# Probability blocks turned by VectorE in 32x32 squares and through a scratch tensor in HBM

## What is computed

```python
h = _layernorm(x, axis=-1) * (1 + ca) + sa          # x: (2, 1024, 256)
qkv = jnp.einsum('bsh,ph->bsp', h, weight_qkv).reshape(b, s, NKV, GROUP)
scores = jnp.einsum('bsgqd,btgd->bgqst', q, k) * scale
scores = jnp.where(causal, scores, jnp.finfo(scores.dtype).min)
attn = jax.nn.softmax(scores, axis=-1)
out = jnp.einsum('bgqst,btgd->bsgqd', attn, v)
x = x + ga * jnp.einsum('bse,he->bsh', out, weight_proj)
```

## Time and profile before

| | us |
|---|---|
| median of three runs | 979.47 (979.19 to 979.89) |
| the profiled execution, its own time | 979.04 |
| its span, first to last instruction | 977.2 |
| PE, PEld busy in the span | 947.1, 816.0 |
| DVE, ACT, POOL busy in the span | 653.1, 516.6, 467.7 |
| mean granted TensorE clock | 0.997 of full |
| DMA over the span | 22 GB/s |

### The profile page before, as it was taken

One profiled execution on the slowest core, in us unless ns is written; L12 is line 12 of the kernel. 1 busy time (PEld: TensorE's weight loads), 2 busy tenths in 40 slices (PEclk: granted clock), 3 DMA queues, 4 the chain that ended last, 5 costly groups with the idle time before them and its releaser, 6 DMA issues.

```text
span 977.2 us, 14506 instructions
## 1 busy us (share of the span) xinstructions
PE 947.1 (97%) x5344; PEld 816.0 (83%) x5344; DVE 653.1 (67%) x1290; ACT 516.6 (53%) x1085; POOL 467.7 (48%) x603
## 2 busy tenths in 40 slices
PE   6899999999999999999999999999999999999997
PEld 5688888888898889888988898889888987888885
DVE  6777657775777577757775777567757776864553
ACT  2466646664666466646664666466646665331221
POOL 3665646564556455545654565456545656120000
PEclk9999999999999999999999999999999999999999
DMA  8000000100010001000000010001000020000000
GB/s 313 24 1 33 2 22 1 33 1 22 1 33 2 22 1 33 1 23 1 33 1 22 1 33 1 22 1 34 1 1 1 1 87 1 1 8 15 21 21 21
DMA packets 9666, 21.92 MB, mean 22 GB/s; under 512 B 1280, under 2 KB 5504, under 8 KB 9472
## 3 DMA queue, kind: packets, MB, share of 16 engines
q1 hardware_dynamic: 8736, 20.45, 6.2%
q10 hardware_dynamic: 864, 0.60, 0.2%
HBM read 18.96 MB, written 2.10 MB: 22 GB/s over the span
## 4 chain that ended last, share of the span: by engine, by line
PE 80%; DVE 9%; ACT 5%; POOL 3%; issue 2%; DMA 1%; SPq 0%; DVEq 0%; POOLq 0%; ACTq 0%
PE ps L801 17%; PE ps L803 16%; PE ps L802 16%; PE ps L924 10%; PE ps L903 6%; PE ps L909 6%; PE ps L906 6%; ACT prob L487 2%; POOL rinv L373 2%; DVE pt_lo L706 2%; POOL prob L378 2%; DVE xhat L614 1%; DVE ps L702 1%; PE ps L825 1%; DVE v_lo L681 1%
## 5 line engine op out<-in xcount | busy, mean ns | idle before, releaser
L706 DVE TENSOR_TENSOR pt_lo<-ps,pt_hi 128x512 fp32r<-128x512 f32 x288 | 198.0, 690 | 101.7 <-ACT pt_hi L506 98.9
L506 ACT ACTIVATE pt_hi<-ps 128x512 fp32r<-128x512 f32 x288 | 171.0, 597 | 134.1 <-PE ps L924 132.6
L373 POOL TENSOR_TENSOR rinv<-rsum,mone 128x1 f32<-128x1 f32 x256 | 140.7, 550 | 211.5 <-ACT prob L487 210.7
L378 POOL TENSOR_SCALAR prob<-prob,rinv 128x1024 f32<-128x1024 f32 (+7 forms) x256 | 192.2, 751 | 53.3 <-POOL rinv L373 53.3
L487 ACT ACTIVATE prob<-ps,nmax 128x1024 f32<-128x1024 f32 (+7 forms) x256 | 189.5, 741 | 50.0 <-DVE nmax L702 48.3
L702 DVE CUSTOM_DVE_ANT_0 ps<-ps,mask_f 128x1024 f32<-128x1024 f32 (+7 forms) x256 | 192.9, 765 | 21.8 <-PE ps L909 19.5
L924 PE MATMUL ps<-ident,prob 128*128 128x128 f32 x1152 | 175.1, 273 | 6.2 <-DVE pt_lo L706 3.6
L924 PEld LDWEIGHTS ps<-ident,prob 128*128 128x128 f32 x1152 | 140.3, 140 | 36.8 <-DVE pt_lo L706 10.9
L801 PE MATMUL ps<-pt_hi,v_hi 128*128 128x512 f32 x288 | 132.5, 460 | 1.3 <-DVE pt_lo L706 0.5
L803 PE MATMUL ps<-pt_hi,v_lo 128*128 128x512 f32 x320 | 126.3, 395 | 0.0
L903 PE MATMUL ps<-k_hi,q_hi 128*128 128x512 f32 (+4 forms) x384 | 117.6, 360 | 0.0
(11 more groups left out here) (134 smaller groups left out, 1575.8 us busy)
## 6 DMA issues: line engine op xcount, KB each, us to landing
w_raw<-in_wqkv SPq DMA_DIRECT2D x9, 768.0 KB, 4.2
wp_raw<-in_wproj SPq DMA_DIRECT2D x8, 512.0 KB, 3.5
x<-in_x SPq DMA_DIRECT2D x4, 512.0 KB, 9.8
prob<-in_wug SPq DMA_DIRECT2D x4, 512.0 KB, 5.3
out_y<-prob SPq DMA_DIRECT2D x4, 512.0 KB, 3.0
prob<-in_wmod SPq DMA_DIRECT2D x1, 1024.0 KB, 9.7
raw_down<-in_wdn SPq DMA_DIRECT2D x1, 1024.0 KB, 14.1
prob<-in_wmod SPq DMA_DIRECT2D x1, 512.0 KB, 5.2
```

The source lines that it names most:

```text
L378: g_.tensor_scalar(row, row, rinv[:, s % 2, h:h + 1], 1.0, ALU.mult, ALU.mult).then_inc(prob_done, 1)
L506: a_.activation(pt_hi[:, n % 3, :], T[n % 2], ACT.Copy).then_inc(pth_done, 1)
L706: v_.tensor_tensor(pt_lo[:, n % 3, :], T[n % 2], pt_hi[:, n % 3, :].bitcast(F32), ALU.subtract).then_inc(ptl_done, 1)
```

## The change

In rows 7, 6 and 5 the last four units (`SWAPPED`, 12 of 36) are no longer transposed by TensorE. For each head of such a row VectorE transposes 32x32 squares of the last four blocks from `prob` into `blocks` (X in the order, placed by a planner `BEHIND` units of its clock after the head's scores). When all four heads are there, SP stores `blocks` (128x2048 numbers) to `spill` in HBM, waits for it, and reads it back in four loads, one for each 32 partitions, which brings the squares to their places in `swapped` (two buffers). In the order such a unit is E instead of T: ScalarE makes `pt_hi` from `swapped` (the first of a row waits for the loads), GpSimd makes `pt_lo`. On ScalarE the held exponentials run after E's work. `pt_hi` and `pt_lo` have four buffers. GpSimd now follows `WALK`, and splits the weights after row 4, head 3. `raw_down` and the butterflies' buffers share memory with `swapped` and `blocks`; the load of `wdn` and its first butterflies move to the end of the last turn.

```diff
+QB = 32
+NB = P // QB
+SWAP_ROWS = [7, 6, 5]
+GROUP = 4
+SWAPPED = [n for n, (i, j) in enumerate(UNITS) if i in SWAP_ROWS and j > i - GROUP]
+TURNED = [n for n in range(NU) if n not in SWAPPED]
...
-    return out
+    return with_blocks([("E", n, 0) if what == "T" and n in SWAPPED else (what, n, h) for what, n, h in out])
+BEHIND = 3300
+WEIGHTS_AFTER = 4
+def with_blocks(walk):
+    cost = {"C": 1360, "VT": 900, "L": 1000, "T": 443, "V": 680, "Y": 1400, "E": 0}
+    out, open_blocks, now = [], [], 0
+    for what, n, h in walk:
+        while open_blocks and now >= open_blocks[0][0]:
+            out.append(open_blocks.pop(0)[1])
+        out.append((what, n, h))
+        now += 160 * (n + 1) if what == "S" else cost[what]
+        if what == "S" and n in SWAP_ROWS:
+            open_blocks.append((now + BEHIND, ("X", n, h)))
+    return out + [block for _, block in open_blocks]
...
+                    for r, i in enumerate(SWAP_ROWS):
+                        at = group(t, i)
+                        sp.wait_ge(block_done, this(block_done, t, QPG * (r + 1)))
+                        if at >= 2:
+                            sp.wait_ge(el_done, len(SWAPPED) + (at - 1) * GROUP)
+                        sp.dma_start(spill[at % 2, :, :], blocks[:, :]).then_inc(spill_s[at % 2], 16)
+                        sp.wait_ge(spill_s[at % 2], (at // 2 + 1) * 16)
+                        for kb in range(NB):
+                            sp.dma_start(swapped[kb * QB:(kb + 1) * QB, at % 2, :].rearrange("p (a n) -> p a n", a=NB),
+                                         spill[at % 2, :, kb * GROUP * P:(kb + 1) * GROUP * P].rearrange(
+                                             "(a p) n -> p a n", a=NB)).then_inc(swap_s[at % 2], 16)
...
+                    def swapped_low(n):
+                        pool.wait_ge(eh_done, this(eh_done, t, SWAPPED.index(n) + 1))
+                        g_.tensor_tensor(by_head(pt_lo, n), swapped_tile(t, n), by_head(pt_hi, n).bitcast(F32),
+                                         ALU.subtract).then_inc(el_done, 1)
+                    for what, i, h in WALK:
+                        if what == "E":
+                            swapped_low(i)
+                        if what == "S":
+                            normalise(i, h)
+                        if what == "S" and (i, h) == (WEIGHTS_AFTER, QPG - 1):
                             pool.wait_ge(wraw_s, (t + 2) * 16)
...
+                        if what == "E":
+                            i, j = UNITS[n]
+                            if n >= 4:
+                                act.wait_ge(pv_done, this(pv_done, t, n - 3))
+                            if j == i - GROUP + 1:
+                                act.wait_ge(*landed(group(t, i)))
+                            a_.activation(by_head(pt_hi, n), swapped_tile(t, n), ACT.Copy).then_inc(eh_done, 1)
                             exps()
...
+                        if what == "X":
+                            s = NT - 1 - n
+                            at = group(t, n)
+                            if h == 0 and at:
+                                dve.wait_ge(spill_s[(at - 1) % 2], ((at - 1) // 2 + 1) * 16)
+                            dve.wait_ge(prob_done, this(prob_done, t, QPG * s + h + 1))
+                            v_.transpose(blocks[:, :].rearrange("p (k j h q) -> p j k h q", k=NB, j=GROUP, h=QPG)[:, :, :, h, :],
+                                         prob[:, s % 2, h, (n + 1 - GROUP) * P:(n + 1) * P].rearrange(
+                                             "p (j k q) -> p j k q", j=GROUP, k=NB)).then_inc(block_done, 1)
...
+                            if n in SWAPPED:
+                                pe.wait_ge(el_done, this(el_done, t, SWAPPED.index(n) + 1))
+                            else:
+                                pe.wait_ge(ptl_done, this(ptl_done, t, turned(n) + 1))
```

More of the change, by code:

```diff
@@ L87, in halves, with build @@
     return (2, n // 2) if n > CH else (1, n)
-def build(nc, x_in, wqkv, wproj, wmod, c_cols, wug, wdn, su_ug, su_dp, ws_ug, ws_dp, ident_in, mask_in, had_in, out):
+def build(nc, x_in, wqkv, wproj, wmod, c_cols, wug, wdn, su_ug, su_dp, ws_ug, ws_dp, ident_in, mask_in, had_in, out, spill):
     ctx = ExitStack()
@@ L109, in build @@
         prob = sb("prob", [P, 2, QPG, SEQ])
-        pt_hi = sb("pt_hi", [P, 3, CH], F32R)
-        pt_lo = sb("pt_lo", [P, 3, CH], F32R)
+        pt_hi = sb("pt_hi", [P, 4, CH], F32R)
+        pt_lo = sb("pt_lo", [P, 4, CH], F32R)
+        blocks = sb("blocks", [P, GROUP * CH])
+        swapped = sb("swapped", [P, 2, GROUP * CH])
+        raw_down = swapped[:, 0, :]
+        sum_dn, dif_dn = (blocks[:, n * 4 * HID:(n + 1) * 4 * HID].rearrange("p (a k n) -> p a k n", a=2, k=KH)
+                          for n in range(2))
         o_hi = sb("o_hi", [P, 2, CH], F32R)
@@ L233, in build, with turned, group, landed @@
         CHUNKS += [("q", h, 1) for h in range(QPG)] + [("q", h, 0) for h in range(QPG)]
+        def turned(n):
+            return TURNED.index(n)
+        def group(t, i):
+            return t * NG + SWAP_ROWS.index(i)
+        def landed(g):
+            return swap_s[g % 2], (g // 2 + 1) * 16 * NB
+        def swapped_tile(t, n):
+            i, j = UNITS[n]
+            tile = swapped[:, group(t, i) % 2, :].rearrange("p (a j h q) -> p a j h q", a=NB, j=GROUP, h=QPG)
+            return tile[:, :, j - i + GROUP - 1, :, :].rearrange("p a h q -> p h a q")
+        def by_head(pt, n):
+            return pt[:, n % 4, :].rearrange("p (h a q) -> p h a q", h=QPG, a=NB)
         def bank(c):
@@ L295, in _ @@
                                  wqkv[bass.ds(g + 1, 1), :, :].rearrange("a p (k n) -> p (a k) n", k=KH)).then_inc(wraw_s, 16)
-            wide = sum(i + 1 for i in STEPS if i >= CT)
+                    for r, i in enumerate(SWAP_ROWS):
[9 more added lines that the diff above has]
+                                             "(a p) n -> p a n", a=NB)).then_inc(swap_s[at % 2], 16)
+            sp.wait_ge(el_done, (TURNS + 1) * len(SWAPPED))
+            sp.dma_start(raw_down, wdn).then_inc(raw_s[4], 16)
+            wide = len([n for n in TURNED if UNITS[n][0] >= CT])
             sp.wait_ge(t_done, this(t_done, TURNS - 1, wide))
@@ L367, in _, with normalise @@
                     ln_low(1, b, g, 0)
[L368 to L379, removed]
+                    def normalise(i, h):
+                        s = NT - 1 - i
+                        e = QPG * s + h
+                        pool.wait_ge(exp_done, this(exp_done, t, e + 1))
+                        g_.tensor_tensor(rinv[:, s % 2, h:h + 1], rsum[:, s % 2, h:h + 1], mone[:, :],
+                                         ALU.pow).then_inc(rinv_done, 1)
+                        pool.wait_ge(rinv_done, this(rinv_done, t, e + 1))
+                        pool.sem_inc(pool_gate, 1)
+                        row = prob[:, s % 2, h, 0:(i + 1) * P]
+                        g_.tensor_scalar(row, row, rinv[:, s % 2, h:h + 1], 1.0, ALU.mult, ALU.mult).then_inc(prob_done, 1)
+                    def swapped_low(n):
[8 more added lines that the diff above has]
+                        if what == "S" and (i, h) == (WEIGHTS_AFTER, QPG - 1):
                             pool.wait_ge(wraw_s, (t + 2) * 16)
@@ L387, in _ @@
                                              ALU.subtract).then_inc(w_ready, 1)
+                        if t == TURNS - 1 and what == "S" and (i, h) == (2, QPG - 1):
+                            pool.wait_ge(raw_s[4], 16)
+                            g_.tensor_tensor(sum_dn, a[:, :, :, 0, :], a[:, :, :, 1, :], ALU.add)
+                            g_.tensor_tensor(dif_dn, a[:, :, :, 0, :], a[:, :, :, 1, :], ALU.subtract).then_inc(fly_s, 1)
             def raw_high(n):
@@ L938, in _ @@
                                 pe.wait_ge(v_lo_s, this(v_lo_s, t, 2))
-                            pe.wait_ge(ptl_done, this(ptl_done, t, n + 1))
-                            three(O[s], v_hi[:, j, :], v_lo[:, j, :], pt_hi[:, n % 3, :], pt_lo[:, n % 3, :],
+                            if n in SWAPPED:
+                                pe.wait_ge(el_done, this(el_done, t, SWAPPED.index(n) + 1))
+                            else:
+                                pe.wait_ge(ptl_done, this(ptl_done, t, turned(n) + 1))
+                            three(O[s], v_hi[:, j, :], v_lo[:, j, :], pt_hi[:, n % 4, :], pt_lo[:, n % 4, :],
                                   j == 0, j == i).then_inc(pv_done, 1)
```

42 lines of the change are left out of this document (22 added, 20 removed).

## The result

| | us |
|---|---|
| changed kernel, median of 4 runs | 1195.3 (1194.04 to 1199.72) |
| kernel before, beside it | 979.33 |
| ratio | 1.2214 (95%: 1.218 to 1.2248) |
| the profiled execution: its own time, its span | 1194.25, 1192.5 |
| mean granted TensorE clock | 0.891 of full (before 0.997) |

The kernel is 216 us slower. The forecast of 1176 was 19 us too low, and the range held the time. First the page: busy time and instructions of each engine, the granted clock in 40 slices of the span (before, 9 in all 40), the chain by engine, three new groups, and the transfers.

A forecast was written before the change was run, and what follows sets the result against it. TensorE, busy for 97% of the span, was taken to bound the kernel. 979 + 198 (eight turns of 30.4 us of waits less 5.6 saved) - 1 for the ends = 1176 us; range 1100 to 1222.

The forecast's parts named there:

- the removal: On TensorE, 96 transposed units at 0.44 us go, 42.2 us; with short waits a turn would be 5.6 us shorter.
- Prices of the new work: Per unit: VectorE's square transposes 0.7 us (highest bound 2.2), ScalarE's upper half 0.65, GpSimd's lower half 1.30.
- The trip: A row's 1 MB to HBM and back: write 4.6 us, read 7.0, together 11.6, bounds 9.3 to 13.5.
- rival 1: Loads into 32 partitions keep the full rate: read 5.6 instead of 7.0 us, 34 us less, 1142; chance 0.18.
- half rate: Loads into 32 partitions run at half the rate: 2.8 us more, read 8.4, kernel 1210; chance 0.15 with beyond.
- The waits: TensorE's waits at swapped units in rows 7, 6 and 5: 30.4 us a turn against 5.6 saved, 198 us in eight.
- The ends: Butterflies moved from start to last turn: up to 3.7 us gained at the start, 2.6 lost later, together -1.
- Full rate: Loads into 32 partitions not slowed: read 5.6 instead of 7.0 us, three trips a turn, 1142 us; chance 0.18.
- Slow squares: VectorE's square transposes take 2.2 us instead of 0.7: 36 us on the chains, 1212 or more; chance 0.08.
- Short trip: Write and read take 5 us together, only the orders remain: 12.8 - 5.6 = 7.2 us a turn, 1036; chance 0.12, shared with too strict an order.
- Faster: Swapped units are split before TensorE reaches them, waits under 5.6 us a turn; fully hidden 933 us; chance 0.02.
- No saving: The removed transposes cost TensorE nothing: 979 + 243 - 1 = 1221 us; chance 0.02.

The follow-up runs named there:

- b4_two_units: Changed kernel swapping only the last two units of the three rows, held exponentials ahead of E's work, weights split after row 3: 967.49 us, ratio 0.9893.
- b1_straight: Changed kernel whose four loads each write 512 columns of all 128 partitions instead of 2048 columns of 32; output not the reference's: 1147.18 us.
- a1: Changed kernel with GpSimd splitting the next turn's weights after row 3, head 3 instead of row 4, head 3: 1154.59 us.
- a2: Changed kernel with ScalarE running the held exponentials before E's work instead of behind it: 1148.61 us.
- a3: Changed kernel with both the later weight split and the exponentials ahead of E's work: 1100.05 us.
- c4_filled: Changed kernel with transposes that nobody reads put on TensorE ahead of the waits at five swapped units: 1162.22 us.
- a4_small: Changed kernel with store and loads moving an eighth of the bytes, instructions and orders kept, output not the reference's: 1112.83 us.
- b2_putback: Changed kernel in which TensorE makes the 12 units' transposes again at E, into a free bank that nobody reads: 1193.86 us.

## Why the prediction was right, and where it was short

**What bounds the kernel, and the removal.** Transposes at 0.44 us a unit were on the path before; `b4_two_units` shows the gain where little waits: a turn of 97.2 us in the mean against 98.8, 1.6 of the 2.6 + 0.3 that six units promise. In the changed kernel the removal is worth nothing more, since waits follow it. The sum took waits that are longer by what is saved, and took the saving off again, which comes to the same.

**Prices of the new work.** A square transpose 705 ns (taken 0.7, from the slower row; all 96 lie between 690 and 714, so the bound of 2.2 fell), the upper half 620 (0.65), the lower half on GpSimd 1265 (1.30).

**The trip.** Store 3.84 us (taken 4.6, bounds 4.4 to 4.9, so outside them), loads 7.25 (7.0, bounds 4.9 to 8.4), together 11.1 against 11.6. The slope from the earlier trace rows, 0.7 us for each 256 KB, was nearly right for the store (2.6, 3.3 and 3.84 us for 512 KB, 768 KB and 1 MB); the base was too high, 3.0 us for 512 KB where `b4_two_units` has 2.6, and the 4.9 came from a load's time. For the loads `b1_straight` shows that the middle was the right choice: 5.7 us without the 32 partitions, which is the 5.6 of rival 1, and 1.6 more with them, where half rate would be 2.8. By the Trainium skill (SBUF — State Buffer, the section on the DMA port swizzle) 32 partitions reach half of the ports, from which I had estimated about 7 us for the read. The 7.25 us measured lies near that estimate, and the 1.6 us over loads into 128 partitions goes in its direction.

**The waits.** Predicted and measured, in us:

| | V(7,4) | V(7,5) | V(6,3) | V(6,4) | V(5,2) | V(5,3) | sum |
|---|---|---|---|---|---|---|---|
| predicted | 6.1 | 2.7 | 8.9 | 0.5 | 5.1 | 7.1 | 30.4 |
| measured | 5.1 | 1.6 | 7.7 | 0 | 3.2 | 6.0 | 23.5 |

(V(7,4) with the 0.83 ahead of V(7,3).) Each place and each releaser is as walked through, the held exponentials and the weights among them; `a1`, `a2` and `a3` show those two by themselves. Each of the five is 1 to 2 us shorter. I read two reasons for it, which no run separates: the store is 0.8 us quicker, and TensorE arrives later, since it runs slower behind each wait. VectorE's stand at X(6,0) was next to nothing: the store landed at 431.58, VectorE ended its work before at about 431.55 and started X(6,0) at 431.60, and the wait ahead of V(7,3) is 0.83 instead of 1.4.

**The term that was missing.** The step that failed is the sum "waits of 30.4 against 5.6 saved: 24.8 us a turn". It holds TensorE's work at the length that it has in the earlier trace rows. It ran 8.8 us longer in the turn: 98.8 - 5.6 + 23.5 + 8.8 = 125.5, measured 125.35 for that turn and 125.8 in the mean. (The 8.8 counts a removed unit at 0.44 us. In `b4_two_units` PE's busy time is 2.0 us a turn lower for six units, which would make it 7.6 with less saved; the sum stays.) `c4_filled` takes the clock out of it: 121.9 us in the mean, 23.1 over the turn of before where I had 24.8. So the walk was 1.7 us a turn too high (14 us), the price of the clock, which I had at nothing, is 3.9 us a turn (33 us between the two medians), and the miss of 19 us is their difference. That I came so close was in part luck: two errors of opposite sign.

**The ends.** The start gained 4.9 us: GpSimd's last scaling of row 7 in the first turn starts at 48.83 instead of 53.69. The two copies of the earlier trace rows take 0.49 us now that no GpSimd pass runs beside them, which answers the 4.34 there:

```profile
25.66 0.49 DVE L743 CAST had_r<-prob 128x256 fp32r<-128x256 f32 x2
```

At the end the butterflies stand on the chain in front of row 1's reciprocal at 1017.90, as predicted from the earlier trace rows:

```profile
1013.18 2.37 POOL blocks L470
1015.54 2.35 POOL blocks L471
```

From that scaling in the last turn to the end it is 262.8 us, before 231.9; less the 27.0 by which a turn is longer, 3.9 are lost (taken 2.6). Both ends together are about -1, as in the sum, with each of them a little larger.

**The rivals.** Full rate (1142): `b1_straight` has the 5.7 us of it and gains 48 us where I had 34; the case is false for loads into 32 partitions, and its price left out the clock. Slow squares: false, at 705 ns. Short trip (1036): false here, and `a4_small` tries its price: it has 14.9 us of waits where I had 12.8, but 1113 us; 77 us off, of which the waits are 8 x 2.1 = 17, and the clock (0.934) and what I can't split make the rest. Faster: false for this kernel; its condition, a sum of waits under what is saved, is met by `b4_two_units`. No saving: the time lies 26 us from its 1221 and 19 from mine, but `b4_two_units`, with a turn 1.6 us shorter than before, rules it out, and `b2_putback` shows why the kernel itself can't tell.

**What was to show it.** PE's share was to be about 77% and is 82%, a turn 123 to 124 us and is 125.8: both because of the slower matmuls. The six places, the pass in front of E(5,3) and the landings 11 us behind the last X were as written.

## What to carry to other kernels

Where engines share one order by hand, a wait on a transfer must be priced with all that stands behind it on the same engine and on the engines that this feeds: here a held exponential and a weight pass made 95 of 216 us, and decided the sign of the smaller version. Compare for every consumer the room (what its engine has to do ahead of it in its own order) with trip plus hand-offs, and shrink the batch until it fits; half the batch together with the two orders turned 1.22 into 0.99, and half the batch alone into 1.03. Add to each wait of TensorE what its lower clock costs afterwards.

## What of the hardware was not expected

- Waits of several us go with a lower granted clock of TensorE (0.62 in the window with V(7,4)'s 4.23 and V(7,5)'s 1.58, 0.52 in the one with V(5,3)'s 6.02; with fillers, and waits of at most 1.7 us left, it is 1.00), and the full work behind them starts on the low level: a V's matmul is 0.43 us on the chain instead of 0.23. Of 8.8 us of longer records a turn only 3.9 are lost time, and useless transposes in the waits win 33 us back.
- Four loads of 256 KB into 32 partitions each take 7.25 us from the first issue to the last landing, and 5.7 as four loads into 128 partitions with the same bytes.
- The store grows slowly with its size: 128 KB 1.9 us, 512 KB 2.6, 768 KB 3.3, 1 MB 3.84.
- VectorE's transposes of 32x32 squares take 705 ns for 128x512 fp32 and 436 ns for 128x256, about as long as the pass of the same size that subtracts out of PSUM (690 ns for 128x512).
